# Second attention of a two-layer block, in another order: reciprocal behind the third later maxima, weighing and output product in halves, score pairs a unit ahead

## The chip, the cores and the metric

The kernel runs on 1 core of one Trainium2 chip. The metric is the device time of one execution in microseconds. A core has five engines that run side by side and wait for each other by semaphores: PE (matmuls; its weight loads have a row of their own, PEld), DVE (vector), ACT (activations), POOL (GpSimd) and SP (here it issues transfers).

## What is computed

Two layers, each an attention of x (16 sequences of 112 rows, 256 wide) over a context (16 of 375 rows) and a feed-forward part. The change lies in the second attention, which has a softmax over 16 heads of 16 columns:

```python
def _L1_xattn_ref(query, key_value, Wq, bq, Wk, bk, Wv, bv, Wo, bo):
    ...
    scores = jnp.einsum('bhqd,bhkd->bhqk', Q, K) / scale
    weights = jax.nn.softmax(scores, axis=-1)
    attn = jnp.einsum('bhqk,bhkd->bhqd', weights, V)
    attn = attn.transpose(0, 2, 1, 3).reshape(B, SQ, H * Dh)
    return attn @ Wo.T + bo
...
x = x + _L1_xattn_ref(_layernorm(x, axis=-1), ctx_1024, L1_xattn_Wq, ...)
```

## The kernel before

The second attention takes one sequence after the other; such a sequence is called a unit here, n = 0 to 15. Nothing is scheduled by a tool: each engine has its own function `step(n)`, and what stands in it is that engine's queue, in that order. An engine that waits holds everything behind it in its queue. A semaphore is read as "wait until event k of unit n has been".

In a unit the 16 heads are gone through twice. First their scores are made with the queries on the partitions, to find each row's maximum; then they are made again transposed, with the keys on the partitions, so that their exponentials can be fed to PE as they stand.

- `score(n, j)` (PE, L2235): scores of two heads, 2 matmuls of 375 columns, j = 0 to 7. Pairs alternate between two sets of banks, so a pair waits for the maxima of the pair two before it. `two_max(n, j)` (DVE, L2070) takes the maxima of such a pair. The pairs of unit n + 1 are made while unit n is worked on; pairs 0 and 1 of unit n + 2 come at the end of unit n.
- `shift_turn(n)` (PE, L2244) transposes all 16 maxima of a unit once the last are there; ACT copies them (`high`, L1965), DVE makes the second half (`shifts`, L2078), ACT spreads both over the heads in 3 copies (`qpk`, L1969). Only then can the transposed scores of unit n start. This is the hand-over from one unit to the next.
- `transposed_scores(n, u)` (PE, L2263): 4 matmuls of 112 columns, u = 0 to 11, over three banks in turn: it waits for the exponential of u - 3. The exponential itself is one ACT instruction (`probs`, L1979) for each u.
- `add_tiles` (POOL, L1886, L1892) adds up the exponentials over the key tiles; `add_up(n, m)` (PE, L2289, 8 matmuls) sums them over the partitions, m = 0 and 1 for half the heads each. `invert_sums` (DVE, L2093) takes the reciprocal.
- `weigh(n, m)` (PE, L2276, 24 matmuls of 32 output partitions, four side by side in the array) multiplies exponentials and values; `normalise` (DVE, L2100) multiplies with the reciprocal into `au`.
- `out_product(n)` (PE, L2301, 4 matmuls in fp32, which the trace shows as 8) multiplies `au` with the output weights into a bank that u = 1, 4, 7, 10 use too; `add_x` (DVE, L2086) adds it to x. The next unit but one may write that bank at u = 1 only after `add_x`.
- `keep_warm` (PE, L2307) is 3 matmuls whose result nobody reads, twice in unit 0. `zero_padded` (ACT, L1932) lays out the values of the next unit behind exponential `PAD_AFTER`.

A matmul on the whole array and one on 32 columns of it are called full and tiled here. `weigh` and `add_up` are tiled, all others full.

Unit 15 has a queue of its own kind: DVE and ACT prepare the feed-forward part there, and `team_rows` (L1603, DVE) normalises the first rows for it at the end of unit 14. PE takes them up at L1701, ahead of unit 15.

Of the kernel before, what the change touches and what calls it, by code (L numbers as in the profile page):

```python
# [29 lines left out]
KC = D // 128  # L30
KT, NKT = 125, 3
# [93 lines left out]
def two_layer_kernel(nc, d, out):  # L125
# [1885 lines left out]
    def _(dve):  # L2011
# [129 lines left out]

        def step(n):
            more = n + 1 < B
            for j in range(1, H // 2):
# [46 lines left out]
    def _(pe):  # L2191
# [75 lines left out]
        def weigh(n, m):  # L2267

            pe.wait_ge(exp1_done.sem, exp1_done.at(n, UNITS // KC * (m + 1)))
            pe.wait_ge(vz_done.sem, vz_done.at(n))  # L2270
            if m == 0 and n:
                pe.wait_ge(au_done.sem, au_done.at(n - 1))
            for e in range(2 * NKT):
                h, t = divmod(e, NKT)
                for g in range(4):
                    ins = pe.matmul(banks[B_PV][32 * g:32 * g + 32, m * SQ:(m + 1) * SQ],  # L2276
                                    vz[:, n % 2, t, 4 * m + g, h],
                                    probs[:, m, t, (2 * g + h) * SQ:(2 * g + h + 1) * SQ],
                                    start=(e == 0), stop=(e == 2 * NKT - 1), tile_position=(0, 32 * g))
            ins.then_inc(pv_ps.sem, 1)  # L2280

        def add_up(n, m):

# [8 lines left out]
            if m == KC - 1:  # L2292
                ins.then_inc(sums_ps.sem, 1)

        def out_product(n):
            pe.wait_ge(au_done.sem, au_done.at(n))
            if n + 2 < B:
                pe.wait_ge(exp1_done.sem, exp1_done.at(n + 1, LAST_IN_PRODUCT + 1))
            for half in range(2):
                for m in range(KC):  # L2300
                    ins = pe.matmul(product_of(n)[:, half], au[:, m], wo1[:, m, half * 128:(half + 1) * 128],  # L2301
                                    start=(m == 0), stop=(m == KC - 1))
            ins.then_inc(wo1_ps.sem, 1)

        def keep_warm():
            for r in range(KEEP_WARM // 2):
                pe.matmul(banks[B_PV][:, 0:D], wo1[:, 0, 0:128], wo1[:, 1], start=True, stop=True)  # L2307

        def step(n):
            more = n + 1 < B  # L2310
            if not more:
                team_turn(pe, 0)
            for u in range(UNITS):
                if n == 0 and u in (0, 3):
                    keep_warm()
                transposed_scores(n, u)
                if u == 0 and n:
                    add_up(n - 1, 1)
                if u == 3 and not more:
                    gates(pe, 0)  # L2320
                if u == 6 and not more:
                    out_product(n - 1)
                if u == 9 and not more:
                    bias_product()
                for j in SCORES_AFTER.get(u, ()):
                    if more:
                        score(n + 1, j)
                    if j == WEIGH_AFTER:
                        weigh(n, 0)
            if not more:  # L2330
                marked(pe, 0)
                weigh(n, 1)
                return
            if n:
                out_product(n - 1)
# [6 lines left out]
            weigh(n, 1)  # L2342

        def bias_product():

# [38 lines left out]
        for n in range(B):  # L2384
            if n == 1:
                pe.wait_ge(tables2_in.sem, tables2_in.at(3 + AHEAD - 1))
            step(n)
# [6 lines left out]
        out_product(B - 1)  # L2394
        first(pe, 0, 3)
        for f in range(1, AHEAD_UNITS):
            second(pe, 0, f)
# [341 lines left out]
```

## Time and profile before

| what | us |
|---|---|
| median of 3 runs | 716.63 |
| lowest, highest | 713.95, 716.72 |
| the profiled execution, its own time | 716.42 |
| its span, first to last instruction | 714.6 |
| busy: PE, DVE, ACT, POOL | 678.2, 519.5, 359.3, 334.1 |

The time of an execution is some 1.8 us longer than the span of its trace. Busy time is a mean over stages with different limits; a share close to 1 does not by itself say that an engine sets the pace. Times in the rows are microseconds from the start of the span.

### The profile page before, as it was taken

Reading aid. Unit: us, or ns where it says so; the run is one execution under the profiler, and the core shown is the slowest. Engines: PE = TensorE matmul, PEld = TensorE weight load, DVE = VectorE, ACT = ScalarE, POOL = GpSimd, SP = SyncE. Lnnn points to the kernel's source line nnn. Section 1 sums busy time; section 2 is a strip of 40 time slices with the busy share of each in tenths; the row PEclk is TensorE's granted clock in tenths of the full one; section 3 lists DMA queues with packets and bytes.
Section 4 is the critical chain, followed back from the end, with each engine's and each line's share of the span. In section 5 each row is a group of like instructions: output and inputs, shape, how many; then the busy total and the mean of one; then the engine's idle time right before and its main releaser. Section 6 shows DMA issues by size and latency. Waiting matters only on the chain.

```text
span 714.6 us, 16405 instructions
## 1 busy us (share of the span) xinstructions
PE 678.2 (95%) x6471; PEld 571.6 (80%) x6471; DVE 519.5 (73%) x1166; ACT 359.3 (50%) x700; POOL 334.1 (47%) x232
## 2 busy tenths in 40 slices
PE   8899999999999999999889999999997999999998
PEld 5678788875568999999776777777676887999998
DVE  5788888888867554432777888888988686948464
ACT  2222122226865646555658787787877243232323
POOL 2333333426965588773336878878776000000000
PEclk9999999999999999999999999999999999999999
DMA  9979000003882587733896876877720000000000
GB/s 293 351 263 68 27 27 27 28 26 101 228 216 83 163 236 222 225 88 59 154 183 150 177 182 154 186 159 154 161 63 2 2 2 14 1 27 1 26 14 27
DMA packets 67676, 81.57 MB, mean 114 GB/s; under 512 B 32930, under 2 KB 56066, under 8 KB 65266
## 3 DMA queue, kind: packets, MB, share of 16 engines
q1 hardware_dynamic: 64210, 72.68, 41.9%
q0 software_dynamic: 2816, 3.67, 2.9%
q10 hardware_dynamic: 576, 4.19, 1.4%
q8 instruction: 51, 0.84, 0.5%
q14 instruction: 23, 0.19, 0.1%
HBM read 60.45 MB, written 19.31 MB: 112 GB/s over the span
## 4 chain that ended last, share of the span: by engine, by line
PE 63%; DVE 11%; ACT 10%; DMA 6%; issue 6%; POOL 4%; SPq 0%; DVEq 0%; POOLq 0%; ACTq 0%
PE psum L1280 7%; PE psum L1297 6%; PE psum L2582 6%; PE psum L900 6%; ACT probs L1979 5%; PE psum L1738 5%; DMA kparts_d<-kp 4%; PE psum L366 4%; PE psum L2263 3%; PE psum L2276 3%; PE psum L2235 3%; PE psum L2301 3%; PE psum L936 2%; ACT qpk L1969 2%; PE psum L1746 2%
## 5 line engine op out<-in xcount | busy, mean ns | idle before, releaser
L2070 DVE TENSOR_REDUCE mx<-psum 112x2 f32<-112x750 f32 x128 | 113.2, 925 | 8.1 <-PE psum L2235 7.6
L1979 ACT ACTIVATE probs<-psum 125x448 f32<-125x448 f32 x192 | 91.1, 559 | 17.2 <-PE psum L2263 16.6
L1886 POOL TENSOR_TENSOR half_sum<-probs 125x896 f32<-125x896 f32 x30 | 62.5, 2082 | 28.2 <-ACT probs L1979 28.2
L900 PE MATMUL psum<-w_parts,c_parts 128*125 128x512 f32 x282 | 71.2, 403 | 2.8 <-DVE kv L656 2.7
L2263 PE MATMUL psum<-qpk,kpk 128*128 128x112 bf16 x768 | 61.2, 215 | 4.3 <-ACT probs L1979 4.2
L900 PEld LDWEIGHTS psum<-w_parts,c_parts 128*125 128x125 f32 x282 | 51.3, 185 | 17.1 <-DVE kv L656 3.7
L2263 PEld LDWEIGHTS psum<-qpk,kpk 128*128 128x128 bf16 x768 | 46.2, 99 | 23.3 <-issue 7.2
L2235 PE MATMUL psum<-kpk,qpk 96*128 96x375 bf16 x256 | 62.2, 325 | 2.4 <-DVE mx L2070 2.2
L1892 POOL TENSOR_TENSOR tile_sum<-half_sum,probs 125x896 f32<-125x896 f32 x30 | 62.9, 2098 | 2.4
L1580 ACT ACTIVATE ctx_all<-psum,cols 128x448 f32<-128x448 f32 (+1 forms) x40 | 22.4, 561 | 80.8 <-PE psum L1746 80.8
L1552 POOL TENSOR_TENSOR rs<-ve,mhalf 112x4 f32<-112x4 f32 (+1 forms) x5 | 4.4, 889 | 108.0 <-DVE ve L1595 108.0
L1280 PE MATMUL psum<-rT,we 128*128 128x224 f32 x256 | 49.8, 353 | 0.0
L2582 PE MATMUL psum<-wo_parts,hs_parts 128*112 128x256 f32 x384 | 48.3, 282 | 1.1 <-DVE hs_parts L2480 0.9
L1280 PEld LDWEIGHTS psum<-rT,we 128*128 128x128 f32 x256 | 47.8, 190 | 0.5 <-ACT ctx_all L375 0.5
L2582 PEld LDWEIGHTS psum<-wo_parts,hs_parts 128*112 128x112 f32 x384 | 46.3, 175 | 2.0 <-DVE hs_parts L2480 1.8
L1692 DVE SCALAR_TENSOR_TENSOR ctx_all<-psum,neg_bi,ctx_all 128x448 f32<-128x448 f32 (+1 forms) x40 | 23.5, 589 | 32.4 <-PE psum L1759 32.0
L558 POOL TENSOR_TENSOR rs<-ve,mhalf 112x2 f32<-112x2 f32 x24 | 19.5, 811 | 57.5 <-DVE ve L701 57.5
L207 PE MATMUL psum<-ctx_all,wk 128*128 128x375 f32 x128 | 44.3, 487 | 0.3 <-ACT logits L483 0.3
L2276 PE MATMUL psum<-probs,vz 125*32 125x112 f32 x1536 | 43.1, 260 | 0.8 <-ACT probs L1979 0.7
L366 PE MATMUL psum<-wv,ctx_all 128*125 128x256 f32 x192 | 43.5, 381 | 0.0
L1217 DVE TENSOR_TENSOR h_low<-psum,h_high 128x448 fp32r<-128x448 f32 x32 | 20.0, 625 | 32.3 <-ACT h_high L1098 32.3
L1095 ACT ACTIVATE psum<-psum,b 128x224 f32<-128x224 f32 x64 | 24.3, 418 | 36.7 <-PE psum L1280 34.7
(259 smaller groups left out, 1636.6 us busy)
## 6 DMA issues: line engine op xcount, KB each, us to landing
we<-in_we SPq DMA_DIRECT2D x12, 1024.0 KB, 5.8
kparts_d<-kp SPq DMA_DIRECT2D x16, 562.5 KB, 5.0
kpk<-kparts_d SPq DMA_DIRECT2D x32, 281.2 KB, 4.4
ctx_all<-in_ctxT SPq DMA_DIRECT2D x16, 375.0 KB, 5.4
kpk<-kparts_d SPq DMA_DIRECT2D x32, 187.5 KB, 5.2
we<-in_we ACTq DMA_DIRECT2D x4, 1024.0 KB, 13.3
kpk<-kparts_d SPq DMA_DIRECT2D x32, 93.8 KB, 4.1
qparts_d<-qp SPq DMA_DIRECT2D x16, 168.0 KB, 4.0
```

Of the source, the lines that this page charges most:

```text
L207: ins = pe.matmul(k_bank(n, m)[:, 0:SK], wk1[:, k, m * 128:(m + 1) * 128], ctx_of(n)[:, k], start=(k == 0), stop=(k == KC - 1))
L366: ins = pe.matmul(flat[0:KT, at + t * D:at + (t + 1) * D], ctx_of(b)[:, k, t * KT:(t + 1) * KT], wv1[:, k], start=(k == 0), stop=(k == KC ...
L900: ins = pe.matmul(banks[B_KV[t]][0:KT, :], parts_of[:, x, k, t * KT:(t + 1) * KT], w_parts[:, k, w], start=(k == 0 and (x, w) == SPLIT[0]) ...
L1280: ins = pe.matmul(banks[B_F[g]][:, (f % 2) * CAP:(f % 2 + 1) * CAP], we1[:, s, k, f * 128:(f + 1) * 128], rT[:, s, k], start=(k == 0), sto ...
L1886: pool.tensor_tensor(half_sum[:, m], probs[:, m, 0], probs[:, m, 1], ALU.add)\
L1892: pool.tensor_tensor(tile_sum[:, m], half_sum[:, m], probs[:, m, 2], ALU.add)\
L1979: act.activation(probs[:, m, t, g * HU * SQ:(g + 1) * HU * SQ], banks[B_ST[u % 3]][0:KT, 0:HU * SQ], ACT.Exp, scale=SCALE)\
L2070: dve.tensor_reduce(mx[:, n % 2, MAX_AT + 2 * j:MAX_AT + 2 * j + 2], psum[0:SQ, first:first + 2, 0:SK], AX.X, ALU.max)\
L2235: ins = pe.matmul(banks[B_S[j % 2] + h][0:WIDE, 0:SK], qpk_wide[0:ROWS, s, at:at + WIDE], kpk[0:ROWS, s, 2 * j + h], start=True, stop=True)
L2263: ins = pe.matmul(banks[B_ST[u % 3]][0:WIDE, c * SQ:(c + 1) * SQ], kpk_wide[:, s, at:at + WIDE], qpk[:, s, h], start=True, stop=True)
L2276: ins = pe.matmul(banks[B_PV][32 * g:32 * g + 32, m * SQ:(m + 1) * SQ], vz[:, n % 2, t, 4 * m + g, h], probs[:, m, t, (2 * g + h) * SQ:(2 ...
L2582: ins = pe.matmul(y_of(i, s), hs_parts[:, x, f, s * SQ:(s + 1) * SQ], wo_parts[:, w, f], start=(f == 0 and (x, w) == SPLIT[0]), stop=(f == ...
```

## The change

No work is added or left out in units 0 to 14; each engine's queue is written in another order. On PE, every score pair of the next unit comes earlier, `weigh(n, 0)` and `out_product` are cut in two with other work between the halves, `add_up` moves, and `shift_turn` comes behind the last transposed scores and `add_up(n, 0)`. On DVE, the reciprocal moves from behind the first of the later maxima to behind the third, directly ahead of `normalise`, and `add_x` goes behind the next unit's first maxima and `shifts`. On ACT, `zero_padded` moves from behind exponential 8 to behind exponential 10. Unit 15 keeps its order.

```diff
-SCORES_AFTER, WEIGH_AFTER = {2: (2,), 3: (3,), 7: (4,), 9: (5, 6), 11: (7,)}, 5
-PAD_AFTER = 8
-INVERT_AT, NORM_AT, TEAM_AT = 2, 4, 3
+PAD_AFTER = 10
+INVERT_AT, TEAM_AT = 4, 3
...
             for j in range(1, H // 2):
                 if j == INVERT_AT:
                     team_ahead(n)
-                if j == INVERT_AT and n:
-                    invert_sums(n - 1)
-                if j == (NORM_AT if more else TEAM_AT) and n:
-                    normalise(n - 1)
-                if more:
-                    two_max(n + 1, j)
-                if j == TEAM_AT and not more:
-                    team_entry()
-            if n and more:
-                add_x(n - 1)
-            if more:
-                shifts(n + 1)
+                    if n:
+                        invert_sums(n - 1)
+                        normalise(n - 1)
+                two_max(n + 1, j)
             if n + 2 < B:
                 two_max(n + 2, 0)
-            elif more:
+            shifts(n + 1)
+            if n:
+                add_x(n - 1)
+            if n + 2 == B:
                 team_rows()
...
+            score(n + 1, 2)
+            if n == 0:
+                keep_warm()
+            transposed_scores(n, 0)
+            transposed_scores(n, 1)
+            score(n + 1, 3)
+            transposed_scores(n, 2)
+            if n:
+                add_up(n - 1, 1)
+            else:
+                keep_warm()
+            transposed_scores(n, 3)
+            score(n + 1, 4)
+            transposed_scores(n, 4)
+            transposed_scores(n, 5)
+            score(n + 1, 5)
+            for u in range(6, 10):
                 transposed_scores(n, u)
...
+            weigh(n, 0, 0)
+            transposed_scores(n, 10)
+            score(n + 1, 6)
+            weigh(n, 0, 1)
+            score(n + 1, 7)
             if n:
-                out_product(n - 1)
+                out_product(n - 1, 0)
             if n + 2 < B:
                 score(n + 2, 0)
+            transposed_scores(n, 11)
+            add_up(n, 0)
             shift_turn(n + 1)
             if n + 2 < B:
                 score(n + 2, 1)
-            add_up(n, 0)
-            weigh(n, 1)
+            if n:
+                out_product(n - 1, 1)
+            weigh(n, 1, 0)
+            weigh(n, 1, 1)
```

PE's queue over one later unit, before, from one transposition of the maxima (`ident,mx`) on. `kpk,qpk` with 128x375 is a score pair, `qpk,kpk` with x4 is one group of transposed scores, `tile_sum` is `add_up`, `probs,vz` is `weigh`, `wo,au` the output product:

```order
L2244 MATMUL psum<-ident,mx 128x112 x2
L2235 MATMUL psum<-kpk,qpk 128x375 x2
L2289 MATMUL psum<-tile_sum,halves 32x112 x8
L2276 MATMUL psum<-probs,vz 32x112 x24
L2263 MATMUL psum<-qpk,kpk 128x112 x4
L2289 MATMUL psum<-tile_sum,halves 32x112 x8
L2263 MATMUL psum<-qpk,kpk 128x112 x8
L2235 MATMUL psum<-kpk,qpk 128x375 x2
...
L2276 MATMUL psum<-probs,vz 32x112 x24
L2235 MATMUL psum<-kpk,qpk 128x375 x2
L2263 MATMUL psum<-qpk,kpk 128x112 x8
L2235 MATMUL psum<-kpk,qpk 128x375 x2
L2301 MATMUL psum<-wo,au 112x128 x4
```

PE's queue in the change, from the four groups of transposed scores u = 6 to 9 to the transposition and the last tiled run:

```order
L2263 MATMUL psum<-qpk,kpk 128x112 x16
L2276 MATMUL psum<-probs,vz 32x112 x12
L2263 MATMUL psum<-qpk,kpk 128x112 x4
L2235 MATMUL psum<-kpk,qpk 128x375 x2
L2276 MATMUL psum<-probs,vz 32x112 x12
L2235 MATMUL psum<-kpk,qpk 128x375 x2
L2303 MATMUL psum<-wo,au 112x128 x2
L2235 MATMUL psum<-kpk,qpk 128x375 x2
L2263 MATMUL psum<-qpk,kpk 128x112 x4
L2291 MATMUL psum<-tile_sum,halves 32x112 x8
L2244 MATMUL psum<-ident,mx 128x112 x2
```

The tiled work (32x112) stood in three runs in a unit, `add_up(n, 0)` with `weigh(n, 1)`, `add_up(n - 1, 1)`, and `weigh(n, 0)`. It now stands in five: both halves of `weigh(n, 0)` and `add_up(n, 0)` are alone among full matmuls.

DVE's queue over the same unit, before and then in the change (`mx` are the maxima of a pair, `shift` is `shifts`, `x_all` is `add_x`, `au` is `normalise`):

```order
L2078 SCALAR_TENSOR_TENSOR shift<-high,lower,psum 32x112
L2070 TENSOR_REDUCE mx<-psum 112x2 x2
L2093 RECIPROCAL rsum<-psum 128x224
L2070 TENSOR_REDUCE mx<-psum 112x2 x2
L2100 TENSOR_TENSOR au<-psum,rsum 128x224
L2070 TENSOR_REDUCE mx<-psum 112x2 x4
L2086 TENSOR_TENSOR x_all<-psum,xb 112x256
```

```order
L2077 SCALAR_TENSOR_TENSOR shift<-high,lower,psum 32x112
L2085 TENSOR_TENSOR x_all<-psum,xb 112x256
L2069 TENSOR_REDUCE mx<-psum 112x2 x3
L2092 RECIPROCAL rsum<-psum 128x224
L2099 TENSOR_TENSOR au<-psum,rsum 128x224
L2069 TENSOR_REDUCE mx<-psum 112x2 x5
```

The number of operations is the same. `add_x` no longer stands between the last maxima and `shifts`, and the next unit's first maxima do instead.

PE's queue at the start of unit 0, before and then in the change (L2307 and L2310 are `keep_warm`):

```order
L2244 MATMUL psum<-ident,mx 128x112 x2
L2235 MATMUL psum<-kpk,qpk 128x375 x4
L2307 MATMUL psum<-wo 128x256 x3
L2263 MATMUL psum<-qpk,kpk 128x112 x12
L2235 MATMUL psum<-kpk,qpk 128x375 x2
```

```order
L2244 MATMUL psum<-ident,mx 128x112 x2
L2235 MATMUL psum<-kpk,qpk 128x375 x6
L2310 MATMUL psum<-wo 128x256 x3
L2263 MATMUL psum<-qpk,kpk 128x112 x8
L2235 MATMUL psum<-kpk,qpk 128x375 x2
```

A third score pair now stands ahead of `keep_warm` and of the first transposed scores.

## Rows read from the trace of the kernel before

**Rows 1.** One line's instructions (L2244): count, min/median/max ns, first and last start.

```profile
L2244 PE MATMUL psum<-ident,mx x32: 257/259/315, 375.1 to 543.2; 112*128 112x112 f32 x32
```

**Rows 2.** Windows: length, busy of PE, PEld, DVE, ACT, POOL; PEclk; DMA.

```profile
375.10:543.10 168.00, 158.98 (x2955) 118.71 (x2955) 144.72 (x186) 131.83 (x276) 133.45 (x75) 1.00 0.68 147
550.00:556.00 6.00, 5.94 (x46) 5.62 (x47) 3.52 (x15) 4.82 (x13) 0.00 (x0) 0.72 0.01 3
```

**Rows 3.** Timeline of PE, one unit: start, length, instructions merged, [idle before <-releaser].

```profile
431.18 0.36 PE L2244 MATMUL psum<-ident,mx 112*128 112x112 f32 x2
431.37 0.49 PE L2235 MATMUL psum<-kpk,qpk 96*128 96x375 bf16 x2
431.79 0.59 PE L2289 MATMUL psum<-tile_sum,halves 125*32 125x112 f32 x16
432.19 1.33 PE L2276 MATMUL psum<-probs,vz 125*32 125x112 f32 x48
433.46 0.37 PE L2263 MATMUL psum<-qpk,kpk 128*128 128x112 bf16 x4
433.76 0.59 PE L2289 MATMUL psum<-tile_sum,halves 125*32 125x112 f32 x16
434.29 0.57 PE L2263 MATMUL psum<-qpk,kpk 128*128 128x112 bf16 x8
...
436.25 0.72 PE L2263 MATMUL psum<-qpk,kpk 128*128 128x112 bf16 x8 [0.16 <-ACT probs L1979]
...
438.18 1.36 PE L2276 MATMUL psum<-probs,vz 125*32 125x112 f32 x48
439.47 0.49 PE L2235 MATMUL psum<-kpk,qpk 96*128 96x375 bf16 x2
...
440.89 1.10 PE L2301 MATMUL psum<-wo,au 128*112 128x128 f32 x8 [0.21 <-ACT probs L1979]
441.82 0.49 PE L2235 MATMUL psum<-kpk,qpk 96*128 96x375 bf16 x2
442.15 0.36 PE L2244 MATMUL psum<-ident,mx 112*128 112x112 f32 x2
```

**Rows 4.** Timeline of PE early in unit 15.

```profile
547.35 0.36 PE L2263 MATMUL psum<-qpk,kpk 128*128 128x112 bf16 x4
547.64 0.59 PE L2289 MATMUL psum<-tile_sum,halves 125*32 125x112 f32 x16
```

**Rows 5.** Timeline of PE, the last six of those output product matmuls.

```profile
441.17 0.82 PE L2301 MATMUL psum<-wo,au 128*112 128x128 f32 x6
```

**Rows 6.** Timeline of ACT, exponentials, and the hand-over copies between two units.

```profile
423.74 3.60 ACT L1979 ACTIVATE probs<-psum 125x448 f32<-125x448 f32 x8 [0.24 <-PE psum L2263]
...
432.23 1.88 ACT L1969 ACTIVATE qpk<-shift 32x448 bf16<-32x448 bf16 x3 [0.41 <-DVE shift L2078]
...
439.16 0.53 ACT L1979 ACTIVATE probs<-psum 125x448 f32<-125x448 f32 x1
```

**Rows 7.** Timeline of DVE in that unit.

```profile
434.42 1.56 DVE L2093 RECIPROCAL rsum<-psum 128x224 f32<-128x224 f32 x1 [0.40 <-PE psum L2289]
...
437.64 0.39 DVE L2100 TENSOR_TENSOR au<-psum,rsum 128x224 f32<-128x224 f32 x1
```

**Rows 8.** Timeline of PE at the start of unit 0.

```profile
375.29 0.81 PE L2235 MATMUL psum<-kpk,qpk 96*128 96x375 bf16 x4
376.30 1.56 PE L2307 MATMUL psum<-wo 128*128 128x256 f32 x6 [0.20 <-DVE qr L2044]
377.70 0.75 PE L2263 MATMUL psum<-qpk,kpk 128*128 128x112 bf16 x12
```

**Rows 9.** Timeline of DVE there.

```profile
376.65 1.78 DVE L2070 TENSOR_REDUCE mx<-psum 112x2 f32<-112x750 f32 x2
```

**Rows 10.** Timeline of all engines at the end of unit 14.

```profile
543.88 2.09 POOL L1892 TENSOR_TENSOR tile_sum<-half_sum,probs 125x896 f32<-125x896 f32 x1
544.17 2.68 DVE L1603 TENSOR_SCALAR ctx_all<-x_all,mv,rs 112x256 f32<-112x256 f32 x2
```

More of the change, by code:

```diff
@@ L2143, in step @@
             more = n + 1 < B
+            if not more:
+                team_ahead(n)
+                invert_sums(n - 1)
+                normalise(n - 1)
+                team_entry()
+                return
             for j in range(1, H // 2):
@@ L2265, in transposed_scores, with weigh @@
             ins.then_inc(st_ps.sem, 1)
[L2267 to L2274, printed above, removed]
+        def weigh(n, m, odd):
+            if not odd:
+                pe.wait_ge(exp1_done.sem, exp1_done.at(n, UNITS // KC * (m + 1)))
+                pe.wait_ge(vz_done.sem, vz_done.at(n))
+                if m == 0 and n:
+                    pe.wait_ge(au_done.sem, au_done.at(n - 1))
+            for t in range(NKT):
                 for g in range(4):
                     ins = pe.matmul(banks[B_PV][32 * g:32 * g + 32, m * SQ:(m + 1) * SQ],
[L2277 to L2280, printed above, removed]
+                                    vz[:, n % 2, t, 4 * m + g, odd],
+                                    probs[:, m, t, (2 * g + odd) * SQ:(2 * g + odd + 1) * SQ],
+                                    start=(t == 0 and not odd), stop=(t == NKT - 1 and odd == 1),
+                                    tile_position=(0, 32 * g))
+            if odd:
+                ins.then_inc(pv_ps.sem, 1)
         def add_up(n, m):
@@ L2293, in add_up, with out_product @@
                 ins.then_inc(sums_ps.sem, 1)
[L2295 to L2303, printed above, removed]
+        def out_product(n, half):
+            if half == 0:
+                pe.wait_ge(au_done.sem, au_done.at(n))
+                if n + 2 < B:
+                    pe.wait_ge(exp1_done.sem, exp1_done.at(n + 1, LAST_IN_PRODUCT + 1))
+            for m in range(KC):
+                ins = pe.matmul(product_of(n)[:, half], au[:, m], wo1[:, m, half * 128:(half + 1) * 128],
+                                start=(m == 0), stop=(m == KC - 1))
+            if half:
+                ins.then_inc(wo1_ps.sem, 1)
         def keep_warm():
@@ L2309, in step @@
         def step(n):
[L2310 to L2315, printed above, removed]
-                transposed_scores(n, u)
[L2317 to L2321, printed above, removed]
-                    out_product(n - 1)
[L2323 to L2331, printed above, removed]
-                weigh(n, 1)
-                return
+            score(n + 1, 2)
[15 more added lines that the diff above has]
+            for u in range(6, 10):
+                transposed_scores(n, u)
+            weigh(n, 0, 0)
[3 more added lines that the diff above has]
+            score(n + 1, 7)
             if n:
-                out_product(n - 1)
+                out_product(n - 1, 0)
             if n + 2 < B:
                 score(n + 2, 0)
+            transposed_scores(n, 11)
+            add_up(n, 0)
             shift_turn(n + 1)
@@ L2340, in step, with last_step @@
                 score(n + 2, 1)
-            add_up(n, 0)
-            weigh(n, 1)
+            if n:
+                out_product(n - 1, 1)
+            weigh(n, 1, 0)
+            weigh(n, 1, 1)
+        def last_step(n):
+            team_turn(pe, 0)
+            for u in range(UNITS):
+                transposed_scores(n, u)
+                if u == 0:
+                    add_up(n - 1, 1)
+                if u == 3:
+                    gates(pe, 0)
+                if u == 6:
+                    out_product(n - 1, 0)
+                    out_product(n - 1, 1)
+                if u == 9:
+                    bias_product()
+                    weigh(n, 0, 0)
+                    weigh(n, 0, 1)
+            marked(pe, 0)
+            weigh(n, 1, 0)
+            weigh(n, 1, 1)
         def bias_product():
@@ L2386, in _ @@
                 pe.wait_ge(tables2_in.sem, tables2_in.at(3 + AHEAD - 1))
-            step(n)
+            if n + 1 < B:
+                step(n)
+            else:
+                last_step(n)
         add_up_last()
@@ L2393, in _ @@
         second(pe, 0, 0)
-        out_product(B - 1)
+        out_product(B - 1, 0)
+        out_product(B - 1, 1)
         first(pe, 0, 3)
```

2 lines of the change are left out of this document (added).

## The prediction, made before the changed kernel ran

> **What bounds the kernel now.** The change touches one stage, so I read that stage. The count of the transpositions of the maxima gives its length: 16 units, the first transposition at 375.1, the last at 543.2 [rows 1], so 15 unit times in 168.1 us, 11.2 on average. The windows over it [rows 2] give busy time by engine: divided by 15, PE 10.6, DVE 9.65, ACT 8.8, POOL 8.9. No engine is full, and PE's busy time counts pipelined matmuls whole, so the pace has to be read from the order of events. The timeline of PE over one later unit [rows 3] shows it: from one transposition (431.18) to the next (442.15) it is 10.97. PE is never idle for long, but in two places it stands before something: transposed scores that need an exponential (436.25, idle 0.16), and the output product, whose bank is free only after exponential 10 (440.89, idle 0.21). Other waits hide behind matmuls that are still counted as running. To find all of them I add up what PE issues.
>
> **PE's own work in a unit, before.** Starts of merged rows give the cost of each kind:
> - transposed scores: 4 matmuls take 0.36 and 12 take 0.75 when they follow each other, so (0.75 - 0.36) / 8 = 0.049 each [rows 3, 8]; 48 of them are 2.36.
> - score pairs: 441.82 to 442.15, 0.33, and (0.81 - 0.49) / 2 = 0.16 for one matmul where 4 follow each other; I take 0.325 a pair [rows 3, 8]; eight are 2.60.
> - transposition: 431.18 to 431.37, 0.20.
> - output product: 440.89 to 441.82, 0.93.
> - tiled runs, from the first tiled matmul to the next full one: 1.67 (431.79 to 433.46), 0.53 (433.76 to 434.29) and 1.29 (438.18 to 439.47), together 3.49. The first has 64 matmuls and the last 48, so one costs (1.67 - 1.29) / 16 = 0.024 and each run has 1.29 - 48 x 0.024 = 0.14 on top: the next full weight load waits for the tiled matmuls to end. Going into a run also costs. After a score pair the first tiled matmul comes 0.42 after the pair's start (431.37 to 431.79), 0.09 more than the 0.325 of the pair. After transposed scores it comes 0.29 after their start with nothing to wait for (547.35 to 547.64) [rows 4], against 4 x 0.049 = 0.20: again 0.09. Three entries are 0.28.
>
> The sum is 2.36 + 2.60 + 0.20 + 0.93 + 3.49 + 0.28 = 9.86. So PE waits 1.11 in 10.97. No order with these three runs could win more than that in a unit.
>
> **The same sum for the change.** Score pairs, transposed scores and the transposition cost the same. The tiled work stands in five runs. `weigh(n, 0)` in halves: each 24 x 0.024 + 0.14 = 0.72, twice 1.44 in place of 1.29. `add_up(n, 0)` alone: 0.53. `add_up(n - 1, 1)`: 0.53. `weigh(n, 1)` alone: 1.29. Together 3.79, with five entries of 0.09 to 0.10 (0.47) 4.26, against 3.77: the two new borders cost 0.49 a unit. The entry into `weigh(n, 1)` now comes behind half an output product, which no row shows; the nearest are the two entries above, and I take their 0.09. The output product itself is bounded from both sides: six of its matmuls took 0.82 and eight 1.10 [rows 3, 5], so the first two took 0.28, while the later ones come (0.82 - 0.27) / 5 = 0.11 apart, with 0.27 for the last to finish. A start after a wait costs 0.06 on top. In the change the first half follows a score pair and the second another, without a wait, so I take 0.87 for both; if each half loses it again it is 0.99. The sum is 2.36 + 2.60 + 0.20 + 0.87 + 4.26 = 10.29.
>
> **What PE still waits for in the change.** Everything from `weigh(n, 0, 0)` to the third group of transposed scores of the next unit stands in a row in which what is waited for is early. The maxima of a pair are ready: the 8 pairs are spread over the unit, and DVE has 10.8 for its 9.65. The hand-over is covered: from the transposition to the first spread copy's start it took 1.05 (431.18 to 432.23), and the copy itself is a third of 1.88, some 1.7 in all [rows 3, 6]; meanwhile PE has a score pair, half a product, all of `weigh(n, 1)` and a pair more, 0.20 + 0.33 + 0.44 + 0.09 + 1.29 + 0.33 = 2.7. That is what the new order hides, and it needs `shifts` not to come late: it now stands behind the next unit's first maxima (0.9, half of 1.78 [rows 9]), which start as soon as the last maxima of the unit are done, while transposition and copy need 0.7 from there. It is late by up to 0.2, inside the cover of 1.0.
>
> The wait that remains is at the exponentials. ACT makes one in (3.60 - 0.53) / 7 = 0.44, of 0.53 from start to end [rows 6], PE makes a group of transposed scores in 0.20, and there are three banks. Follow them from u = 3, which no longer waits because `add_up(n - 1, 1)` stands before it: call its start 0. Then u = 4 starts after 0.20 + 0.325 = 0.52 and ends 0.36 later, 0.88; I allow 0.04 for the hand-over, so its exponential starts at 0.92 and ends at 1.45. The next two end at 1.89 and 2.33. u = 9 needs the last of these and, with 0.05 for the way back, starts at 2.38. Without a wait PE would be there after 2 x 0.325 + 6 x 0.197 = 1.83. So PE waits 0.55, and the unit takes 10.29 + 0.55 = 10.84; with unrounded terms I get 10.82, 0.14 to 0.15 less than 10.97. I checked the way of reckoning on the order before: stepping through it with the same durations and hand-over delays (0.04 from PE to ACT or DVE, 0.05 to 0.16 from ACT to PE, the latter the idle time at 436.25) gives 10.96 for a unit where the trace has 10.97, and 167.5 for the fifteen where it has 168.1.
>
> The reciprocal's move costs nothing: 1.56 [rows 7], now after three maxima; `normalise` (0.39, at 437.64 before) ends some 0.4 before `weigh(n, 0, 0)` needs its bank. What covers it is the wait at the exponentials. `zero_padded` moves with it into ACT's wait for u = 11, which PE reaches late, and so no longer delays exponential 9. SP's loads hang on the same groups of transposed scores as before and are three units ahead.
>
> **The ends of the stage.** Unit 0 becomes slower. A third score pair now stands ahead of everything and needs maxima that DVE makes only behind `shifts(0)` (from 376.65, 1.78 for two [rows 9]), so done at about 377.6. PE has issued the two other pairs by 376.0 (375.29 and 0.65) and stands still for 1.6; then come that pair, 0.33, `keep_warm`, which with what it delays takes 1.40 (376.30 to 377.70), and the first transposed scores, which before started at 377.70 [rows 8]: now at 377.65 + 0.33 + 1.40 = 379.4, 1.7 later. A part is hidden, since ACT was not ready at once before either; stepping through, the unit ends 1.27 later. Unit 1 then wins 0.78 of it back. The ten later units of the regular kind give 10 x 0.14 = 1.4. In the last three intervals, where DVE and ACT also split weights, one loses 0.15, one wins 0.34 and one loses 0.13. At the end of unit 14, `team_rows` took 2.68 for two instructions on as many elements as `normalise` has in 0.39 [rows 7, 10], while POOL's last sums ran beside it until 545.97. I take it that DVE waited for POOL there and will again, so that this end comes only as much earlier as the unit does; if it did not, some 1.9 more would be won, 713.7.
>
> Sum: +1.27 - 0.78 - 1.4 - 0.1 = -1.0. Against the profiled execution's 716.42 that is 715.4; the median of the runs shown is 0.2 above that execution, so 715.6.
>
> **Rivals.** What a measurement of this kernel can tell from no change is 0.5%, 3.6 us: below 713.0 or above 720.2. From 715.6, over fourteen units, that is 0.19 a unit less than I reckon or 0.33 more.
>
> *PE loses more at its new borders, and the kernel gets slower.* In the change PE sets the pace except for 0.55, so what its queue costs counts in full, where before 1.11 of waiting took it up. Before half of the short runs stands a separate wait instruction. Where such a wait ended last, PE stood 0.16 before transposed scores [rows 3]. If two of the new borders cost 0.15 each and both product halves lose 0.06, a unit is 0.42 longer than I reckon, 11.25, and 715.6 + 14 x 0.42 = 721.5. It decides from 0.33. Against it: where these waits have long been satisfied, as at 431.79, no such gap is seen. 0.12.
>
> *The borders are free and the change wins much.* By the rows they cost 0.14 and 0.09 each. If a border cost half of it in the change, five times 0.23 would become 0.58 less, a unit 10.25, still above DVE's 9.65: 715.6 - 14 x 0.58 = 707.5. The trace speaks against it at three runs of every unit; a smaller error, 0.19 a unit, gives 712.9. 0.10 for all of this. The Trainium skill, TensorE: Matmul & The Clock Gate, on packing small matmuls (The mechanism), says that PE pulls weight loads ahead of running matmuls where row groups don't conflict or the background buffer is free. By that rule this rival would be right; the rows between tiled and full matmuls do not show it, their weight load comes only near the end of the matmul before.
>
> *The start is not won back, or the clock falls.* In the window 550 to 556, after two idle gaps of PE, the granted clock was 0.72 on average, a part of it at the lower of the two levels (1.2 GHz), and PE worked there at half speed [rows 2]; over the rest of the stage it was 1.00. Unit 0 now has an idle stretch of 1.6. If the clock fell there, or unit 1 won nothing back, 0.8 to 1.5 would be added: 716.4 to 717.1. 0.12. No change beyond what is measured either.
>
> **Numbers.** 0.66 for the forecast, 715.6, alone from 713.5 to 717.4 (0.14 a unit either way). Faster by over 0.5% 0.09, within 0.83, slower 0.08, with a part of each outer rival falling inside. The range reaches from the small form of the second rival, 712.9, to 719.3, where the first one's two waits are there and the product loses nothing, less a part: 0.26 a unit.
>
> **What the profile after would show.** Right: transpositions 10.8 apart in the later units; the first transposed scores of unit 0 at about 379.4 and `keep_warm` at 378.0; five tiled runs, of 0.72 for the halves; waits of PE before u = 7, 8 and 9 on exponentials, and none before the output product. Wrong: a distance of 11.2 or more, with gaps of PE at the new borders; or 10.5 or less. The prediction falls if PE's queue costs 0.3 a unit more or 0.2 less than 10.3, or if ACT takes longer than 0.44 for an exponential beside the denser work of PE.

## The result, and the profile after

The change takes 720.87 us (median of 11 executions, 718.57 to 724.68) where the kernel before takes 716.63 (11 executions on the same chip, 712.15 to 718.73). The ratio is 1.0066, with a 95% interval of 1.004 to 1.0091: slower by 0.4 to 0.9%. The forecast was 715.6 and the range ended at 719.3, so the prediction was wrong, on the side of its small chance of 0.08. The profiled execution of the change took 718.80, with a span of 717.0, 2.4 more than the span before. It is among the fastest of the eleven and has the highest mean clock of them (0.995, where most have 0.988): the medians differ by 4.2, the profiled executions by 2.4, and the profile can explain only the latter.

The view of one line's instructions, for the transposition, answers to [rows 1]:

```profile
L2244 PE MATMUL psum<-ident,mx x32: 259/273/318, 373.6 to 545.4; 112*128 112x112 f32 x32
```

The stage starts 1.49 earlier here; nothing ahead of it was changed, so that is a difference between executions. From the first transposition to the last it takes 171.67 where it took 168.00, 3.67 more, and what follows the last takes 171.75 for 171.52. That is the whole difference of the two profiles: -1.49 + 3.67 + 0.23 = 2.4. The next step is to split the stage by its transpositions. Interval n lies between the starts of two of them and holds PE's unit n. These are worked out from the timelines of PE, in us:

| interval | 0 | 1 | 2 to 10 | 11 | 12 | 13 | 14 |
|---|---|---|---|---|---|---|---|
| before | 11.60 | 11.39 | 10.97, once 11.18 | 11.67 | 10.97 | 11.84 | 11.60 |
| the change | 12.91 | 10.50 | 10.92, once 11.81 | **15.01** | 11.12 | 11.55 | 11.38 |
| forecast of the difference | +1.27 | -0.78 | -0.14 each | -0.14 or +0.15 | +0.15 or -0.14 | -0.34 | +0.13 |
| measured | +1.31 | -0.89 | -0.05 each | +3.34 | +0.15 | -0.29 | -0.22 |

The prediction puts the +0.15, -0.34 and +0.13 into "the last three intervals". Read by the letter these are 12 to 14, and 11 is one of the ten regular ones. I meant 11, 13 and 14, the three that were irregular before, but the record doesn't show it. By either reading interval 11 was to lose 0.15 at most. One interval holds 3.34 of the 3.67. The timeline of PE there:

```profile
501.80 1.42 PE L2263 MATMUL psum<-qpk,kpk 128*128 128x112 bf16 x14
505.67 0.78 PE L2276 MATMUL psum<-probs,vz 125*32 125x112 f32 x24 [2.45 <-DVE au L2099]
...
507.01 1.34 PE L2276 MATMUL psum<-probs,vz 125*32 125x112 f32 x24
508.29 0.81 PE L2235 MATMUL psum<-kpk,qpk 96*128 96x375 bf16 x2
508.89 1.06 PE L2303 MATMUL psum<-wo,au 128*112 128x128 f32 x4
```

Two things are to be seen. Before the first half of `weigh(n, 0)` PE stands still for 2.45 and waits for DVE's `au`, that is `normalise`. Behind it the second half takes 1.34 instead of 0.78, a score pair 0.81 instead of 0.49. The windows (length; busy of PE, PEld, DVE, ACT, POOL; granted clock; DMA) say why: from 507.00 to 510.40 the granted clock is 0.50, the lower of the two levels (1.2 GHz). By the windows it fell at 506.97, 1.30 after PE had started again.

```profile
503.60:507.00 3.40, 1.33 (x30) 0.88 (x30) 3.31 (x4) 0.71 (x3) 3.36 (x2) 1.00 0.94 163
507.00:510.40 3.40, 3.40 (x34) 2.50 (x34) 2.00 (x3) 1.28 (x3) 0.75 (x1) 0.50 0.02 5
510.40:513.80 3.40, 3.40 (x79) 2.71 (x78) 2.55 (x4) 2.29 (x5) 2.34 (x2) 1.00 0.47 130
```

Why `au` is late stands in the timelines of DVE and of POOL:

```profile
500.82 0.74 DVE L1585 BATCH_NORM_STATS2 st<-x_all 112x6 f32<-112x256 f32 x2
...
501.88 1.71 DVE L1594 TENSOR_SCALAR ve<-mv 112x2 f32<-112x2 f32 x1
503.50 1.54 DVE L2092 RECIPROCAL rsum<-psum 128x224 f32<-128x224 f32 x1
505.14 0.39 DVE L2099 TENSOR_TENSOR au<-psum,rsum 128x224 f32<-128x224 f32 x1
```

```profile
501.48 2.08 POOL L1885 TENSOR_TENSOR half_sum<-probs 125x896 f32<-125x896 f32 x1 [1.76 <-ACT probs L1978]
```

L1594 adds a constant to two numbers in each of 112 partitions, and takes 1.71. It ends at 503.59, when POOL's sum has ended at 503.56. In the profile before the same instruction took 0.17:

```profile
499.87 0.75 DVE L1586 BATCH_NORM_STATS2 st<-x_all 112x6 f32<-112x256 f32 x2
...
500.94 0.17 DVE L1595 TENSOR_SCALAR ve<-mv 112x2 f32<-112x2 f32 x1
501.02 1.56 DVE L2093 RECIPROCAL rsum<-psum 128x224 f32<-128x224 f32 x1
```

There POOL did nothing between 500.20 and 502.00:

```profile
499.45 0.75 POOL L1879 TENSOR_TENSOR xb<-x_all,rows 112x256 f32<-112x256 f32 x1
502.00 2.08 POOL L1886 TENSOR_TENSOR half_sum<-probs 125x896 f32<-125x896 f32 x1 [1.80 <-ACT probs L1979]
```

The DVE instructions from BATCH_NORM_STATS2 to the addition are the part of `team_ahead` that only unit 11 has, the row statistics for the feed-forward part. The change moves them together with the reciprocal (`if j == INVERT_AT: team_ahead(n)`, and `INVERT_AT` went from 2 to 4), to a place directly ahead of reciprocal and `normalise`, while POOL adds up the first exponentials.

My theory was then: the new order of the regular units is about as good as forecast; what costs is `team_ahead` at its new place, first by its own 1.1, then by DVE being held while POOL's sum runs, then by the clock that falls behind PE's idle stretch. The rivals: the new start, which is 1.3 slower; the borders of the tiled runs; and a clock that falls for another reason.

### The profile page after: what moved, and what is told of

It is laid out like the page before. It is cut to its first block and busy times, and to the rows that moved or that the text cites. A ratio compares the mean times of both kernels' runs of the same rounds, so it can differ in the third digit from the quotient of the medians.

```text
span 717.0 us, 16407 instructions
## 1 busy us (share of the span) xinstructions
PE 682.2 (95%) x6471; PEld 574.0 (80%) x6471; DVE 521.0 (73%) x1166; ACT 361.1 (50%) x700; POOL 333.9 (47%) x232
## 3 DMA queue, kind: packets, MB, share of 16 engines
q0 software_dynamic: 2816, 3.67, 2.9%
## 5 line engine op out<-in xcount | busy, mean ns | idle before, releaser
L2069 DVE TENSOR_REDUCE mx<-psum 112x2 f32<-112x750 f32 x128 | 115.1, 933 | 16.7 <-PE psum L2235 15.9
L2263 PE MATMUL psum<-qpk,kpk 128*128 128x112 bf16 x768 | 63.7, 215 | 2.8 <-ACT probs L1978 0.8
L2276 PE MATMUL psum<-probs,vz 125*32 125x112 f32 x1536 | 47.4, 264 | 3.9 <-DVE au L2099 2.5
L2276 PEld LDWEIGHTS psum<-probs,vz 125*32 125x32 f32 x1536 | 35.8, 110 | 13.0 <-issue 8.7
```

The source lines that it names most:

```text
L2069: dve.tensor_reduce(mx[:, n % 2, MAX_AT + 2 * j:MAX_AT + 2 * j + 2], psum[0:SQ, first:first + 2, 0:SK], AX.X, ALU.max)\
L2263: ins = pe.matmul(banks[B_ST[u % 3]][0:WIDE, c * SQ:(c + 1) * SQ], kpk_wide[:, s, at:at + WIDE], qpk[:, s, h], start=True, stop=True)
```

## The experiments

Eight kernels ran. Ratios are against the kernel before on the same chip, with the 95% interval; each kernel has one profile, and times of intervals are read from it.

### The statistics back at their old place

```diff
-                if j == INVERT_AT:
+                if j == 2:
                     team_ahead(n)
-                    if n:
-                        invert_sums(n - 1)
-                        normalise(n - 1)
+                if j == INVERT_AT and n:
+                    invert_sums(n - 1)
+                    normalise(n - 1)
```

> The change with one thing undone: the row statistics for the feed-forward part (team_ahead, run in unit 11, and the weight splits in units 14 and 15) stand behind the first of the later maxima again, not directly ahead of the reciprocal. Theory 1 (the loss sits in unit 11, where the statistics delay reciprocal, normalise and weighing, PE then stands idle 2.45 and its clock falls): interval 11 between transpositions falls from 15.01 to 11.3 to 11.6, the low clock at 507 is gone, the kernel is 3.3 to 3.7 faster than the change, 717.0 to 717.6 by the medians. Theory 2 (the denser PE queue loses by itself, at borders and by low clocks all along): interval 11 still falls, but the median stays above 719, since most executions of the change show lower clocks than the profiled one.

Measured: 715.94 (12 executions) against 718.26 (30), ratio 0.998 (0.9951 to 1.0008). Interval 11 is 11.37 instead of 15.01, and the stage takes 167.52. DVE and PE in unit 11:

```profile
500.62 0.17 DVE L1594 TENSOR_SCALAR ve<-mv 112x2 f32<-112x2 f32 x1
500.70 1.78 DVE L2069 TENSOR_REDUCE mx<-psum 112x2 f32<-112x750 f32 x2
502.39 1.55 DVE L2092 RECIPROCAL rsum<-psum 128x224 f32<-128x224 f32 x1
504.03 0.39 DVE L2099 TENSOR_TENSOR au<-psum,rsum 128x224 f32<-128x224 f32 x1
```

```profile
504.57 0.78 PE L2276 MATMUL psum<-probs,vz 125*32 125x112 f32 x24 [0.31 <-DVE au L2099]
...
505.91 0.78 PE L2276 MATMUL psum<-probs,vz 125*32 125x112 f32 x24
```

Interval 11 is in the range expected, and the median lies 1.1 below the expected 717.0, beside a kernel before that took 718.26 there and not 716.63. One `if` takes the whole loss back. The stage is 0.48 shorter than in the profile before, where the sum had promised 1.0; 0.21 of the 0.48 is the one irregular unit of the kernel before (11.18). What is missing is mostly in the regular units (10.92, not 10.82).

### That, and the start of unit 0 as before

```diff
 # on top of the edit above
-            score(n + 1, 2)
-            if n == 0:
+            if n:
+                score(n + 1, 2)
+            else:
                 keep_warm()
             transposed_scores(n, 0)
             transposed_scores(n, 1)
+            if n == 0:
+                score(n + 1, 2)
```

> As e1_team_early, and in unit 0 alone the third score pair stands behind the second transposed scores, not ahead of keep_warm. Theory 1: interval 0 falls from 12.9 to 11.6, unit 1 stays at 10.5, so 1.3 less than e1_team_early, about 716. Theory 2: the idle time at the start matters for the clock too, more than 1.3 is won against e1_team_early. If neither start nor statistics matter, it stands at the change's 720.9.

Measured: 717.03 (12), ratio 0.999 (0.9957 to 1.0023). Intervals 0 and 1 are 11.67 and 10.67, together 22.34 for 23.40 with the slower start, so the start costs 1.06 (1.24 by the last experiment, whose interval 1 is 10.49); but interval 6 is 11.44, an irregular unit, and the stage takes 167.00, 0.52 less where 1.3 was expected. The start is a real cost of 1.1 to 1.2 and not the cause: this version is not measurably faster than the first one, which keeps the slower start.

### The statistics late, but no DVE instruction that POOL can hold

```diff
-        dve.tensor_scalar(ve1[:, i % 2, 0:g], mv1[:, i % 2, 0:g, 1], EPS, None, ALU.add)\
-            .then_inc(fve_done.sem, 1)
+        if i:
+            dve.tensor_scalar(ve1[:, i % 2, 0:g], mv1[:, i % 2, 0:g, 1], EPS, None, ALU.add)\
+                .then_inc(fve_done.sem, 1)
...
             if n == TEAM_STATS:
+                pool.wait_ge(f_stats.sem, 2)
+                pool.tensor_scalar(ve1[:, 0, 0:2], mv1[:, 0, 0:2, 1], EPS, None, ALU.add)\
+                    .then_inc(fve_done.sem, 1)
                 inverse_root(pool, 0)
```

> The change, but the last instruction of the row statistics in unit 11 (112x2 elements, adding a constant, L1594 on DVE, 1.71 long while POOL's sum of exponentials ran) is done by POOL in its own queue. The statistics stay at the late place. Theory 1a (DVE was held by POOL's running instruction): DVE's reciprocal starts 1.5 to 1.7 earlier, PE's idle time before weighing in unit 11 falls from 2.45 to 0.7 to 1.0, no low clock there, interval 11 is 12.2 to 12.8: 2.2 to 2.8 faster than the change. Theory 1b (the statistics are simply long at that place, whatever POOL does): the reciprocal starts 0.2 earlier and interval 11 stays above 14.

Measured: 720.16 (12), ratio 1.0006 (0.9977 to 1.0034). Interval 11 is 11.84, still shorter than the 12.2 to 12.8 expected. The reciprocal starts 0.03 behind the last statistics (503.14), although POOL's sum runs beside it, and PE's idle time is 0.84 instead of 2.45, with no fall of the clock:

```profile
503.17 1.56 DVE L2096 RECIPROCAL rsum<-psum 128x224 f32<-128x224 f32 x1
```

```profile
502.77 2.08 POOL L1886 TENSOR_TENSOR half_sum<-probs 125x896 f32<-125x896 f32 x1 [1.75 <-ACT probs L1982]
```

```profile
505.35 0.78 PE L2280 MATMUL psum<-probs,vz 125*32 125x112 f32 x24 [0.84 <-DVE au L2103]
```

The wait for the statistics (`f_stats`) still stands ahead of the reciprocal here, so it is not that wait which took the 1.71. The place of the statistics alone costs 11.84 - 11.37 = 0.47 of interval 11. The rest of the 3.64 (15.01 - 11.37) hangs on the one instruction.

### The kernel before, with its statistics put late

```diff
-                if j == INVERT_AT:
+                if j == (NORM_AT if more else TEAM_AT):
                     team_ahead(n)
```

> The kernel before with the row statistics moved behind the third later maxima, directly ahead of normalise, and nothing else of the change. Theory 1: the place of the statistics alone costs, since weighing waits for normalise there too: interval 11 grows from 11.67 to 12.5 if POOL is idle at that moment and to 13.5 to 15 if POOL's sum is running, interval 14 grows by 0.5: 1.3 to 4 slower than before. Theory 2: within 0.5 of before, since PE has over 1 us of waiting in a unit to take it up.

Measured: 724.32 (7), ratio 1.0072 (1.0045 to 1.01). Nothing else of the change is in this kernel. Interval 11 is 15.77 for 11.67, PE stands idle for 2.72 there, and the clock is low when it starts again (a mean of 0.54 from 507.60 to 513.40). The same instruction is held at a later sum of POOL, while the statistics themselves, which also read SBUF beside a sum, keep their 0.75 (rows of POOL and of DVE, in order of time):

```profile
502.96 2.08 POOL L1886 TENSOR_TENSOR half_sum<-probs 125x896 f32<-125x896 f32 x1 [1.81 <-ACT probs L1979]
504.42 0.75 DVE L1586 BATCH_NORM_STATS2 st<-x_all 112x6 f32<-112x256 f32 x2
505.12 2.08 POOL L1892 TENSOR_TENSOR tile_sum<-half_sum,probs 125x896 f32<-125x896 f32 x1
...
505.49 1.73 DVE L1595 TENSOR_SCALAR ve<-mv 112x2 f32<-112x2 f32 x1
```

In unit 14 the weight splits, which `team_ahead` also holds, meet POOL here and interval 14 becomes 17.43, with a low clock from 547.1, before PE starts again at 547.84:

```profile
542.54 2.08 POOL L1886 TENSOR_TENSOR half_sum<-probs 125x896 f32<-125x896 f32 x1 [2.72 <-ACT probs L1979]
...
543.05 2.13 DVE L1535 TENSOR_TENSOR wi_first<-ctx_all,wi_first 128x512 fp32r<-128x512 f32 x1
```

All three came out above what was expected: interval 11 (13.5 to 15), interval 14 (0.5 more, measured 5.83) and the median (1.3 to 4 more, measured 6.1). The ratio is like that of the change, but the sum behind it is not: here interval 11 loses 4.10 and interval 14 another 5.83, where the change loses 3.34 and wins 0.22. So this run shows that the place alone costs and how, not that it costs the same.

### The change, with PE busy in the idle stretch

Ten matmuls whose result nobody reads stand ahead of `weigh(n, 0, 0)` in unit 11; they are work that the reference doesn't need.

```diff
+            if n == TEAM_STATS:
+                pe.wait_ge(exp1_done.sem, exp1_done.at(n, 8))
+                for r in range(10):
+                    pe.matmul(banks[5][:, 0:128], wo1[:, 0, 0:128], wo1[:, 1, 0:128], start=True, stop=True)
             weigh(n, 0, 0)
```

> The change with 10 matmuls that nobody reads on PE in unit 11, ahead of the first half of weighing, some 2.2 long, where PE stands idle for 2.45. Nothing else is changed, normalise is as late as in the change. Theory 1c (part of the loss is the low clock that follows the idle time): no low clock at 507, interval 11 falls from 15.01 to 14.0 to 14.4, and the executions show a mean clock above the change's 0.990. Theory 1d (the idle time itself is the whole loss, the low clock hides behind other waits): interval 11 stays within 0.2 of 15.0.

Measured: 721.43 (12), ratio 1.0022 (0.9995 to 1.005). Interval 11 is 13.49, 1.52 less than in the change and less than the 14.0 to 14.4 expected, with the clock at 1.00 throughout the interval; the executions have a mean clock of 0.993, where the change's have 0.990. The unread matmuls fill the stretch up to the same late `au`, which starts 8.94 behind the transposition here and 8.95 in the change:

```profile
508.20 2.50 PE L2334 MATMUL psum<-wo 128*128 128x128 f32 x20
510.63 0.78 PE L2276 MATMUL psum<-probs,vz 125*32 125x112 f32 x24
```

```profile
508.20:511.60 3.40, 3.40 (x49) 3.11 (x50) 3.31 (x5) 0.82 (x2) 3.32 (x3) 1.00 1.00 200
```

This divides the 3.64 between the change and the first experiment in interval 11: 15.01 - 13.49 = 1.52 is the clock; 13.49 - 11.84 = 1.65 is DVE's wait for POOL (it was held 1.71 - 0.17 = 1.54); 11.84 - 11.37 = 0.47 is what the statistics cost more at the late place, unheld. The parts are read from one profile each. The ratios over all executions (1.0066, 1.0022, 1.0006 and 0.998) fall in the same order, and the intervals of the change and of the third experiment lie apart; those of neighbours overlap, so they don't confirm the single sizes.

### The tiled runs: `weigh(n, 0)` in one piece

```diff
 # on top of the first experiment
             weigh(n, 0, 0)
+            weigh(n, 0, 1)
             transposed_scores(n, 10)
             score(n + 1, 6)
-            weigh(n, 0, 1)
             score(n + 1, 7)
```

> e1_team_early with the first weighing of a unit in one piece again (both halves behind u = 9, then u = 10 and score pairs 6 and 7). One border less, 0.24 of PE's work saved a unit. If PE's own work sets the unit, 10.92 becomes 10.7. If instead the delay of u = 10 and of score pair 6, and with it of the last maxima, sets it, the unit becomes 11.15 to 11.3 and the kernel 3 to 4 slower than e1_team_early.

Measured: 721.51 (10), ratio 1.0025 (0.9996 to 1.0055). A regular unit takes 11.20, as expected, 0.28 more than with halves, although it has one border less: what comes later by it, `u = 10` and score pair 6, costs more. DVE stands still for 0.64 before the last three maxima of such a unit, where in the change it is 0.20 before the last two. PE goes through the whole run in 1.29, the step (439.61 to 440.90) that the sum used:

```profile
439.61 1.36 PE L2276 MATMUL psum<-probs,vz 125*32 125x112 f32 x48
440.90 0.37 PE L2263 MATMUL psum<-qpk,kpk 128*128 128x112 bf16 x4
```

Besides, interval 0 was 15.16 in this profile, with a low clock (0.50) in the window from 375.80 to 379.20, behind the idle stretch of 1.64 at the slower start. That is 2.24 more than the 12.92 of the first experiment. So that start can cost the clock as the prediction's third rival had it; in the change's own profile it didn't.

### The reciprocal alone at its early place

```diff
 # on top of the first experiment
-                if j == INVERT_AT and n:
+                if j == 2 and n:
                     invert_sums(n - 1)
+                if j == INVERT_AT and n:
                     normalise(n - 1)
```

> e1_team_early with the reciprocal alone behind the first of the later maxima, where it was before; PE's order is that of the change, so the sums that it needs come 1 us later in the unit than before. If the reciprocal's place is free, as the prediction has it for the move, the unit stays at 10.92. If the queue behind it counts, DVE waits for the sums, the maxima behind it come late, PE's score pairs wait for them, and PE reaches the sums late: 13.2 a unit, some 27 more in all.

Measured: one execution, 756.35, so no interval can be given. Regular units take 13.26 to 13.27 at best and 14.25 or more where the clock falls, which it does eight times in the stage. DVE waits 1.91 for the sums, which in the new order come later than the first maxima, and the other maxima stand behind it:

```profile
477.74 0.93 DVE L2069 TENSOR_REDUCE mx<-psum 112x2 f32<-112x750 f32 x1
...
480.58 1.56 DVE L2092 RECIPROCAL rsum<-psum 128x224 f32<-128x224 f32 x1 [1.91 <-PE psum L2292]
```

The unit was expected to within 0.1, the time was not (some 27 more expected, 40 found): the stretches of low clock, which were not in the reckoning, lengthen eight intervals by about 1 or more. The reciprocal's move is what makes the new order of PE possible at all; what must not move with it is `team_ahead`.

### The version put together from these

The start of unit 0 as before; the statistics at j = 2, but the weight splits at the late place, where interval 14 is shorter.

```diff
 # on top of the second experiment
-                if j == 2:
+                if j == (2 if n == TEAM_STATS else INVERT_AT):
                     team_ahead(n)
```

> The change with unit 0's third score pair behind the second transposed scores, the row statistics of unit 11 behind the first later maxima, and the weight splits of units 14 and 15 at the change's late place. It puts together what the first runs showed to be better. Theory 1 (place of the statistics and start are all that the change loses): intervals 11.6, 10.6, ten of 10.92, 11.4, 11.1, 11.55, 11.4: 166.6 to 167.0 from first to last transposition against 168.0 before, 0.4 below e3_team_and_start, median 1 to 1.5 below the kernel before. Theory 2 (the denser queue brings low clocks of its own): median not below before.

Measured: 717.21 (12) against 719.31 (29), ratio 0.9976 (0.9957 to 0.9995). It is the only version whose interval lies below 1: some 0.2% faster than the kernel before. It is also the best of eight and the upper end is 0.9995, so the gain is barely clear of noise. The stage takes 166.5, with intervals 0 and 1 at 11.67 and 10.50, interval 11 at 11.37 and interval 14 at 11.38 where the first experiment has 11.78; one unit was irregular (11.54).

## Why the prediction was wrong

**The step that failed** is "The reciprocal's move costs nothing". The prediction prices the move by the reciprocal's own 1.56 in a regular unit and names its cover, but not what else the same `if` holds. `team_ahead` went along, and no sentence of the prediction names it. The sum has for interval 11 either the regular -0.14 or the "one loses 0.15"; the runs show +3.34. The parts above add up to 3.64 because they count from the first experiment, whose interval 11 is 0.30 shorter than before. Undoing the move of `team_ahead` alone gives 0.998 for 1.0066, and doing it alone to the kernel before gives 1.0072, the latter with a second loss in unit 14.

**The mechanism was on the page.** The prediction read the 2.68 of L1603 in [rows 10] as DVE waiting for POOL's last sums, and used it only for the end of unit 14. L1594 is the same form of instruction, and POOL's timeline of before has sums under way from 502.00 on, one behind the other, which is where the statistics went. The cover was also thinner than the 0.4 of the prediction: in a regular unit `au` ends at 436.41 and PE starts `weigh(n, 0, 0)` at 436.72, 0.31 later. Where PE waits for `au` the hand-over itself takes 0.14 (505.53 to 505.67 in the change), so about 0.16 is left, and whatever delays DVE by more goes to the end of the unit in full. The runs bear this out: `au` starts 6.26 behind the transposition in a regular unit, 6.87 in unit 11 of the first experiment and 7.33 in that of the third, 0.61 and 1.07 later, and these intervals are 0.45 and 0.92 longer than 10.92. The Trainium skill, SBUF — State Buffer, Who interferes with whom, names `tensor_scalar` among the DVE operations that can, when their operands meet its conditions, take the port pair shared with GpSimd, which is then held for a whole instruction while the other engine is fully blocked. Here the trace agrees: L1594 ended 0.03 behind POOL's instruction, however small it is; the reciprocal, which reads PSUM, was not held beside the same sum (503.17 above).

**Rivals.** The third one had the clock right and its place wrong: in the change's profile it falls in unit 11, not in unit 0, and costs 1.52 on top of the 2.12 that DVE's delay itself costs. The first, that PE's borders cost more, was wrong: there is no gap at them in a regular unit. That its time, 721.5, lies near the measured 720.87 is an accident. The second, that they cost half, was wrong too.

**What was right.** The order of a regular unit, here from 435.27 to the next transposition and the run behind it:

```profile
435.27 1.52 PE L2263 MATMUL psum<-qpk,kpk 128*128 128x112 bf16 x16
436.72 0.78 PE L2276 MATMUL psum<-probs,vz 125*32 125x112 f32 x24
437.44 0.37 PE L2263 MATMUL psum<-qpk,kpk 128*128 128x112 bf16 x4
437.64 0.49 PE L2235 MATMUL psum<-kpk,qpk 96*128 96x375 bf16 x2
438.06 0.78 PE L2276 MATMUL psum<-probs,vz 125*32 125x112 f32 x24
438.78 0.50 PE L2235 MATMUL psum<-kpk,qpk 96*128 96x375 bf16 x2
439.11 0.60 PE L2303 MATMUL psum<-wo,au 128*112 128x128 f32 x4
439.55 0.49 PE L2235 MATMUL psum<-kpk,qpk 96*128 96x375 bf16 x2
...
440.68 0.41 PE L2244 MATMUL psum<-ident,mx 112*128 112x112 f32 x2
440.93 0.49 PE L2235 MATMUL psum<-kpk,qpk 96*128 96x375 bf16 x2
```

The halves take 0.72 each (436.72 to 437.44, 438.06 to 438.78). The first half of the product takes 0.44 (439.11 to 439.55) without a wait, so 0.87 for both is right and 0.99 is not. The wait at the exponentials is there: u = 6 to 9 take 1.45 (435.27 to 436.72), where 16 x 0.049 + 0.09 = 0.87 would do, so 0.58, against 0.55 reckoned.

**What was mis-sized.** A regular unit takes 10.92, not 10.82, and wins 0.05, not 0.14 to 0.15. Of the 0.10, 0.05 is the transposition, which takes 0.25 behind a tiled run (440.68 to 440.93) and not the 0.20 of [rows 3], where it stood behind a full one, and 0.03 the longer wait above; the last 0.02 is spread over steps that differ by no more than the rounding of the rows. (The 168.1 that the prediction has for the stage before counts to the second matmul of the last transposition; from start to start it is 168.00.) The ten regular units were to win 1.4; the regular ones won 0.05 each.

**The start** was right. The transposed scores begin 4.28 behind the first transposition, and 4.3 was forecast; `keep_warm` 2.98, forecast 2.9; PE stands still 1.64 before the pair, forecast 1.6:

```profile
373.58 0.38 PE L2244 MATMUL psum<-ident,mx 112*128 112x112 f32 x2 [0.49 <-DVE mx L2069]
373.80 0.81 PE L2235 MATMUL psum<-kpk,qpk 96*128 96x375 bf16 x4
376.24 0.48 PE L2235 MATMUL psum<-kpk,qpk 96*128 96x375 bf16 x2 [1.64 <-DVE mx L2069]
376.56 1.46 PE L2310 MATMUL psum<-wo 128*128 128x256 f32 x6
377.86 0.56 PE L2263 MATMUL psum<-qpk,kpk 128*128 128x112 bf16 x8
```

The end of unit 14 was right as well: `team_rows` is held again, 2.54 for its two instructions from 546.69 on, with POOL's last sum under way until 548.33.

**Left open.** In the change's profile one `weigh` run breaks off for 0.61 with nothing that the profile shows to wait for, and interval 6 takes 11.81:

```profile
441.79 1.05 PE L2276 MATMUL psum<-probs,vz 125*32 125x112 f32 x33
443.44 0.59 PE L2276 MATMUL psum<-probs,vz 125*32 125x112 f32 x15 [0.61 <-issue]
```

The kernel before has one such unit too (interval 4, 11.18), and so have four of the experiments (11.26 to 11.54); the first, the third and the one with `weigh` whole have none. Where it shows, its place goes with the order of PE's queue: the run of `weigh(5, 1)`, in interval 6, in all four profiles of the new order that have it, and `add_up(3, 1)`, in interval 4, in both profiles of the old one. Its length differs, and no run shows what it is.

Interval 12 takes 11.12 in most versions with the new order. The trace shows where its 0.20 over a regular unit arises, though not why: DVE stands still for 0.44 between the reciprocal and `normalise` with nothing that the profile shows to wait for, so `au` (517.82) starts 6.62 behind the transposition and not 6.26. In the third experiment, where the interval takes 10.92, it does not.

## What to carry to other kernels

When a call moves, list everything that its branch issues, the calls of one unit alone too, and price each at its new neighbours: for DVE's constant additions and its operations on two SBUF tensors, look at what POOL runs there. A tiny one can cost nearly a whole POOL instruction. Here the statistics themselves and what reads PSUM were not held. Where an engine waits about 2 us in such a place, add what the clock takes behind it; the idle stretch on PE was worth 1.5 more than its own length here. And before taking a duration from another place, see what stood ahead of it: a full matmul behind a tiled run is not the one behind a full run.

## What the runs showed of the hardware

- An addition to 112x2 numbers on DVE took 0.17 with POOL idle, 1.71 (the change) and 1.73 (its statistics' late place in the kernel before) with a POOL sum of 2.08 under way; a 128x512 split of two SBUF tensors 0.68 alone (L1534, the change, 538.49) and 2.13 beside one (L1535, 543.05 above). Two BATCH_NORM_STATS2 took 0.74 in the change, where POOL was idle for nearly all of it, and 0.75 beside a sum (504.42 above).
- The granted clock fell to 0.50 behind PE's idle stretch of 2.45 in unit 11, from 506.97 to 510.39, and this cost 1.52. It did not fall behind the 1.64 at the start in the change's profile, and it did at the same place in the one with `weigh` whole, whose queue up to there is the same. So the same idle stretch, in the same queue, may cost the clock in one execution and not in another.
- The mean clock of an execution goes with its time: of the executions of the kernel before beside the first experiment (29, without the slowest), those with 0.988 to 0.991 took 720.2 to 722.6, those with 0.998 took 713.8 to 718.3. The change's eleven had a mean of 0.990, those 29 one of 0.995. So stretches of low clock probably make up a part of the change's loss beyond the profile's 2.4; in which units they fell in the executions without a profile, no run shows.
